# Mask seeded into the score banks by ScalarE, and value products issued earlier, in the first wide attention

## What is computed

```
q = layernorm(x) @ Wq      # 16 heads of 128
k = ctx @ Wk; v = ctx @ Wv # 8 key/value heads of 128, each used by 2 query heads
scores = q @ k.T / sqrt(128)
scores = where(mask, scores, -inf)   # mask: one flag per batch and context token
attn = nan_to_num(softmax(scores))
x = x + (attn @ v) @ Wo
```

## Time and profile before

| what | us |
|---|---|
| median of 3 runs (lowest, highest) | 3921.48 (3912.77, 3925.12) |
| the profiled execution | 3921.73 |
| its span, first to last instruction | 3920.0 |
| first and last mask product, from the span's start | 42.6, 827.5 |
| PE busy, of the span | 3488.9 (89%) |
| DVE busy | 2466.2 (63%) |
| ACT busy | 1568.4 (40%) |

### The profile page before, as it was taken

One profiled execution on the slowest core, in us unless ns is written; L12 is line 12 of the kernel. 1 busy time (PEld: TensorE's weight loads), 2 busy tenths in 40 slices (PEclk: granted clock), 3 DMA queues, 4 the chain that ended last, 5 costly groups with the idle time before them and its releaser, 6 DMA issues.

```text
span 3920.0 us, 62127 instructions
## 1 busy us (share of the span) xinstructions
PE 3488.9 (89%) x23602; PEld 2816.6 (72%) x23602; DVE 2466.2 (63%) x4698; ACT 1568.4 (40%) x3367; POOL 1284.9 (33%) x1204
## 2 busy tenths in 40 slices
PE   6999999976999579997999789997789999999874
PEld 5788888865777346655998545554579999999854
DVE  6677777764222368865443456665567777777658
ACT  2455554331111045551222245553245555555430
POOL 0003333302242387742222346664322222222202
PEclk9999999997999789998999889999899999999987
DMA  3226666213644111001010100000000000000001
GB/s 116 70 95 209 212 214 196 66 44 150 227 183 183 72 31 27 21 5 55 33 44 1 36 3 4 4 3 16 27 6 17 12 17 17 17 17 6 1 14 43
DMA packets 94406, 246.55 MB, mean 63 GB/s; under 512 B 14369, under 2 KB 18593, under 8 KB 89249
## 3 DMA queue, kind: packets, MB, share of 16 engines
q1 hardware_dynamic: 87872, 222.12, 16.5%
q0 software_dynamic: 6240, 20.45, 1.5%
HBM read 364.95 MB, written 70.52 MB: 111 GB/s over the span
## 4 chain that ended last, share of the span: by engine, by line
PE 36%; DVE 7%; issue 3%; POOL 2%; ACT 2%; DMA 1%; SPq 0%; DVEq 0%; POOLq 0%; ACTq 0%
PE banks L94 32%; PE banks L193 4%; DVE cWK L2660 1%; DVE cm L2658 1%; ACT P L68 1%; POOL rs L77 1%; DVE xn L82 0%; DVE XL L77 0%; POOL kst L77 0%; DVE X L77 0%; POOL X L77 0%; DVE st L230 0%; DVE P L81 0%; DVE PL L77 0%; ACT nkT L71 0%
## 5 line engine op out<-in xcount | busy, mean ns | idle before, releaser
L77 DVE TENSOR_TENSOR X<-X,banks 128x512 f32<-128x512 f32 x352 | 240.4, 684 | 158.5 <-PE banks L94 158.5
L88 DVE TENSOR_REDUCE nmx<-banks 128x4 f32<-128x1024 f32 (+2 forms) x256 | 239.3, 956 | 158.6 <-PE banks L94 155.5
L77 POOL TENSOR_TENSOR slo<-sraw,shi 128x512 fp32r<-128x512 f32 x96 | 125.0, 1302 | 509.1 <-ACT shi L71 509.1
L94 PE MATMUL banks<-XH,wqh 128*128 128x256 f32 x1024 | 290.1, 283 | 0.0
L94 PE MATMUL banks<-XL,wqh 128*128 128x256 f32 x1024 | 283.9, 277 | 0.0
L94 PE MATMUL banks<-XH,wql 128*128 128x256 f32 x1024 | 283.4, 277 | 0.0
L94 PE MATMUL banks<-XH,tT 128*128 128x256 f32 x1024 | 246.2, 284 | 13.7 <-issue 6.6
L94 PE MATMUL banks<-XL,tT 128*128 128x256 f32 x1024 | 245.0, 283 | 0.0
L68 ACT ACTIVATE nPT<-banks 128x1024 f32<-128x1024 f32 x192 | 195.9, 1020 | 110.3 <-PE banks L94 108.6
L94 PE MATMUL banks<-woh,OH 128*128 128x512 f32 x512 | 220.3, 430 | 11.6 <-DVE OL L77 9.2
L94 PE MATMUL banks<-WU,exh 128*128 (+1 forms) x624 | 209.3, 407 | 16.2 <-DMA WU<-expert_parts 14.7
(11 more groups left out here) (389 smaller groups left out, 10487.8 us busy)
## 6 DMA issues: line engine op xcount, KB each, us to landing
WU<-expert_parts SPq DMA_DIRECT2D x39, 4096.0 KB
WD<-expert_parts SPq DMA_DIRECT2D x39, 2048.0 KB
sraw<-in_moe_w SPq DMA_DIRECT2D x96, 256.0 KB, 3.4
expert_parts<-shi SPq DMA_DIRECT2D x96, 256.0 KB
expert_parts<-slo SPq DMA_DIRECT2D x96, 256.0 KB
wqr<-in_L_xattn_Wq SPq DMA_DIRECT2D x16, 512.0 KB, 3.8
wor<-in_L_xattn_Wo SPq DMA_DIRECT2D x16, 512.0 KB, 4.7
sraw<-in_L_ffn_factors SPq DMA_DIRECT2D x32, 256.0 KB, 3.2
```

What stands on the lines that cost most here:

```text
L77: return self.e.tensor_tensor(out, a, b, op)
L88: return self.e.tensor_reduce(out, a, AX.X, op, **kw)
L94: return self.e.matmul(out, l, r, start=start, stop=stop, skip_group_check=skip)
```

## The change

The first layer's steps go by "QT0SP1NE" now: "pv" of unit u comes ahead of "out" (u-1, 1). The two mask products stay for unit 0 alone. For every later unit ACT copies the mask's values into banks 2 and 3 right after the four exponentials of the unit before, and PE's score products, which start no new sum, add to what ACT wrote. PE waits for a new semaphore, seed, where it waited for exp. mrow has 128 partitions now, so DVE's one instruction that makes it writes 128 rows instead of 1. No other stage changes.

```diff
-            for step in "Q0TL1SPNE" if not l0 else "QT0S1PNE":
+            for step in "Q0TL1SPNE" if not l0 else "QT0SP1NE":
...
-            sb("mrow", [1, T], BF16)
+            sb("mrow", [128, T], BF16)
...
                         if u == 0:
                             pe.wait_ge(S["dve_one"], ONE["onesb"])
-                        pe.wait_ge(S["exp"], 4 * U - 2 + 2 * qt)
-                        mb = w["mrow"][0:1, 256 * b:256 * b + 256].unsqueeze(1).to_broadcast([1, 2, 256])
-                        pe.mm(z[:].rearrange("p (h n) -> p h n", h=2), w["onesb"][:], mb, True, False, True)
+                            mb = w["mrow"][0:1, 0:256].unsqueeze(1).to_broadcast([1, 2, 256])
+                            pe.mm(z[:].rearrange("p (h n) -> p h n", h=2), w["onesb"][:], mb, True, False, True)
+                        pe.wait_ge(S["seed"], 2 * (u - 1) + qt + 1)
...
+                if l0 and u < 63:
+                    c = 256 * ((u + 1) % 8)
+                    for qt in range(2):
+                        act.wait_ge(S["exp"], 4 * U + 2 * qt + 2)
+                        act.acopy(banks[2 + qt][:].rearrange("p (h n) -> p h n", h=2),
+                                  w["mrow"][:, c:c + 256].unsqueeze(1).to_broadcast([128, 2, 256])).then_inc(S["seed"], 1)
...
-            dve.ts(w["mrow"][:], w["mu8"][0:1, :], 1.0, 1e30, ALU.subtract, ALU.mult).then_inc(S["dve_one"], 1)
+            dve.ts(w["mrow"][:], w["mu8"][:], 1.0, 1e30, ALU.subtract, ALU.mult).then_inc(S["dve_one"], 1)
```

## The result

The changed kernel takes 3879.26 us in the median (3874.16 to 3884.57, 4 runs), against 3917.12 before (3912.30 to 3925.12, 4 runs of it by then): a ratio of 0.9902, with an interval of 0.9882 to 0.9922. That is 38 us faster. The forecast was 3870, 51.5 faster; the range, 3850 to 3895, holds the time. The execution profiled first is the shortest of its four, with a span of 3872.3 us, and the one of the second series has 3878.4; both are used, the first unless said otherwise. One thing holds for every run here: all flags of the mask are set in these inputs, so every seed that ScalarE writes is 0. The times are those of the full work, but no run shows that a seed of another value would be added to the scores rightly.

A forecast was written before the change was run, and what follows sets the result against it. PE was taken to set the pace of the first attention. From the profiled 3921.7 us, 63.0 came off for mask products and 11.5 was given back for waits, clock effects cancelling: 3870, range 3850 to 3895 (78%).

The forecast's parts named there:

- The saving on PE: First attention: two mask products leave PE's queue, 1.00 us a unit, 63.0 us over 63 units.
- Rival (a): Gaps around the mask product stay with the score products; saving only 0.46 a unit, 29 us, result 3904; chance 8%.
- The copies of ACT: ACT's 126 mask copies into PSUM, 1.08 us a unit, 68 us in all, delay nobody: cost taken 0.
- The 1.44 us by which DVE's chain is later: Moving "pv" puts DVE's addition to X and all behind it 1.44 us later at the next unit, against PE.
- the waits of 1.86: PE idles 1.86 us for QL before the scores in units 20, 28, 36 and 44: 7.4 us of 11.5 given back.
- "On PE nothing" for the move of "pv": Moving "pv" costs PE 0: the same products in another order, with PL ready 0.6 us in time.
- "With some of the small delays in ordinary units": Allowance in the forecast range: up to 0.2 us in 50 ordinary units, 10 us.
- the 0.06 us of room for QL: In ordinary units PE sees QL 2.21 us after the turn, the score product could start at 2.27: wait taken 0.
- cover for the seeds: ACT's idle 0.47 us waiting for sraw in unit 28, counted as 0.5 of what hides the 1.08 of copies.
- The clock: New waits may lose 0 to 9 us, units 1 to 5 may gain 0 to 8; taken to cancel.
- (c): QL comes late in ordinary units too; PE stops before the scores, 42 units cost 130 us: 4000; chance 3%.
- (d): Waiting for seed takes the mask product's place as ACT is late; result within 0.3% of now; chance 3%.

The follow-up runs named there:

- e10: The kernel before, with both operands of the mask product 128 rows deep instead of 1, in bfloat16; 3884.5 us in one run.
- e3: The changed kernel with neither mask products nor ACT's seed copies, in the new order; 3875.9 us, ratio 0.9894.
- e4: The changed kernel with DVE's two weight subtractions (wql, wol) put one at a time behind the scores of two units; 3862.3 us, ratio 0.9864.
- e2: The kernel before with the new step order alone, both mask products still on PE and no seeds; 3934.5 us, ratio 1.0054.
- e5: The changed kernel in the old step order, DVE adding "out" (u-1, 0) to X between the halves of PL from unit 6; 3865.7 us, ratio 0.9866.
- e7: e4 with the load of the next head pair's weights spread over three units; 3860.0 us, ratio 0.9855.
- e11: The kernel before, with both operands of the mask product 128 rows deep and in float32r; 3887.3 us in one run.

## Why the prediction was right, and where it was off

- **The saving on PE** (63.0): right, 1.67 from "out" to the value products as in the last layer's rows. e10 explains it: the pair of products needs 0.44, and being one row deep cost 0.56 more. Rival (a), 29 us, is out.
- **The copies of ACT** (0): right, by e3, whose ordinary unit and waits without them are the same; the 2 us in units 24 and 32 that e3 leaves open are taken up below.
- **The 1.44 us by which DVE's chain is later, and the waits of 1.86 that it brings** (11.5 in all): right in place, mechanism and sum (11.1 and 12.8). QL came at 3.91 for 4.00. Unit 52's wait grew by 0.79 us in the first profile and by 1.93 in the second, where 1.44 was forecast. e4 takes the waits away by taking the 2.4 us of the subtractions out of the chain; e2 brings them with the order alone. The price of one depends on whether POOL works beside the multiplications of P (12.5 to 13.4 in e2).
- **"On PE nothing" for the move of "pv"**: this is the step that failed, a term sized at 0 that is 0.09 to 0.12 us in every unit. It shows in the 24 products that make Q for the next unit. The tenth and the nineteenth of them in unit 27, before and then after:

```profile
410.43 0.28 PE L94 MATMUL banks<-XH,wqh 128*128 128x256 f32 x1
...
411.45 0.28 PE L94 MATMUL banks<-XH,wqh 128*128 128x256 f32 x1
```

```profile
384.83 0.28 PE L94 MATMUL banks<-XH,wqh 128*128 128x256 f32 x1
...
385.89 0.28 PE L94 MATMUL banks<-XH,wqh 128*128 128x256 f32 x1
```

Nine products take 1.02 us before and 1.06 after: some 0.114 and 0.118 each. Before, this faster step holds from the sixth product on; after, all run at 0.118. The ordinary unit is 11.11, not 11.02: 4.5 us. e2, e3 and e5 pin it on the order. What in the engine makes this difference stays open.

- **"With some of the small delays in ordinary units" (up to 10, taken 0)**: 3.5 us, but not where I looked (the 0.06 us of room for QL held). 1.9 of it are in units 24, 32 and 40, which follow the fetch of the next head pair's weights: ACT waits for sraw ahead of OH or of the exponentials, and the chain behind is late. I had put ACT's wait for sraw down as cover for the seeds (0.47 in unit 28); in these units it is itself what comes last. e7 shows it. The other 1.5 are waits for QL and P in units 53 to 55, which the second profile hasn't; their cause stays open.
- **The clock**: letting gains and losses cancel was a guess, and it came out a little low. 4.2 and 2.7 us were gained in units 1, 2, 3 and 5 of the two profiles, where the granted clock stayed at 1.00 in three units and in two. In unit 52 the span at a lower clock costs an estimated 1.67 us in the first profile, as before (1.66), and 3.49 in the second (length of the unit times what its mean clock lacks to 1.00). The waits of units 20, 28, 36 and 44 (up to 1.7 us) didn't bring the clock down in either profile.
- **Rivals (c) and (d)**: from unit 6 to 61 no wait for the seeds, and one of 0.2 us for P; out.

The sum: 51.5 forecast, 46.9 found in the first profile's units, 43.4 in the second's, and 35 to 38 in the medians. The terms named account for 5 to 8 us of the difference; the rest is the spread between profiled and median executions of either kernel, and stays unassigned. There is some luck in the level: the forecast of 3870 starts from 3921.7, which is 4.6 above the median before as it stands now (3917.12). From that median the same terms give 3865.6, 13.7 below what was measured and not 9; it would lie in the range still.

## What to carry to other kernels

Where one engine is busy all the time, the worth of an instruction is the distance between the starts of its neighbours with and without it, and a stage of the same kernel that lacks it gives that number directly. When such an engine gets shorter units, write down for each engine that feeds it when its result was ready and when it will be wanted, in the heaviest unit, not in the ordinary one: here the largest part of what was given back (11.1 of some 20 us) lay in the units with extra work, and moving that work, into idle time that the change itself had made, brought another 17 us on top of the 38 of the change. Before moving a product to another engine, look at whether it is expensive only by its form: the one-row product cost more than twice what the same product over 128 rows did, and deepening it alone brought some 31 us.

## What the runs showed of the hardware that was not expected

- A stream of float32r products of 128 rows on TensorE is held up by a product of one row: a pair with 512 columns took 1.00 us, the same pair with 128 rows 0.44 in bfloat16, and with a period within 0.02 us of that in float32r (rows 4, e10, e11).
- Products of 256 columns in float32r ran with 0.118 us from start to start through all 24 of a projection in one order, and with 0.114 from the sixth on in the other, at the same granted clock; the order of the products ahead of them decides (11.02 against 11.11, 12.02 against 12.14).
- DVE's four multiplications of P took 1.14 us alone (e2) and 2.16 to 2.18 us with POOL's subtraction beside them (rows 6, unit 28 above), so moving them by a microsecond can double them.
- ScalarE wrote 128x512 floats from bfloat16 into PSUM in 0.61 us while TensorE worked in other banks, and none of the 126 copies showed up as a wait of TensorE. Whether products without a start flag add to a seed other than 0 is not shown.
